# Product 4 of the W_base stage formed for two pairs at once, by seven inner products

## The reference

```
q    = relu(cond @ W3 + b3)                        # one row per batch
y    = relu(((512 * x + sum of x over tokens) * q) @ W2 + b2)
g    = softmax(y @ W_router + b_router); the two largest of 6 are kept
out  = x + y @ W_base + b_base + (y @ A_s) @ B_s + sum over e of g_e * (y @ A_r[e]) @ B_r[e]
```

## Time and profile before

| what | value |
|---|---|
| median of 3 runs | 1394.6 us (1394.54 to 1394.91) |
| profiled execution, first to last instruction (span) | 1392.4 us |
| PE busy | 1388.2 us, 6105 matmuls |
| DVE busy | 986.5 us (71%) |
| ACT busy | 644.2 us (46%) |
| DMA queues | 237.78 MB, mean 171 GB/s |

### The profile page before, as it was taken

One profiled execution on the slowest core, in us unless ns is written; L12 is line 12 of the kernel. 1 busy time (PEld: TensorE's weight loads), 2 busy tenths in 40 slices (PEclk: granted clock), 3 DMA queues, 4 the chain that ended last, 5 costly groups with the idle time before them and its releaser, 6 DMA issues.

```text
span 1392.4 us, 18247 instructions
## 1 busy us (share of the span) xinstructions
PE 1388.2 (100%) x6105; PEld 1142.9 (82%) x6105; DVE 986.5 (71%) x1648; ACT 644.2 (46%) x1190; POOL 60.7 (4%) x136
## 2 busy tenths in 40 slices
PE   9999999999999999999999999999999999999999
PEld 6888888888888888888888888888888888888887
DVE  6987777676786757768889667766667656586663
ACT  7774756657465564655544232431314313243130
POOL 3000110000000000000000001000000000000000
PEclk9999999999999999999999999999999999999999
DMA  8243836445264452546836549556463665635542
GB/s 318 75 168 113 263 122 182 156 122 165 62 184 153 122 165 61 171 130 211 285 92 195 212 132 342 176 190 226 146 239 114 203 213 167 218 107 175 211 155 87
DMA packets 146429, 237.78 MB, mean 171 GB/s; under 512 B 39872, under 2 KB 40128, under 8 KB 146336
## 3 DMA queue, kind: packets, MB, share of 16 engines
q1 hardware_dynamic: 135680, 199.75, 43.6%
q0 software_dynamic: 9792, 35.66, 8.3%
q10 hardware_dynamic: 864, 1.22, 0.2%
HBM read 157.53 MB, written 79.04 MB: 170 GB/s over the span
## 4 chain that ended last, share of the span: by engine, by line
PE 100%; DVE 0%; DVEq 0%; issue 0%
PE ps L2392 33%; PE ps L2393 33%; PE ps L2394 33%; PE ps L2403 1%; PE ps L2418 0%; PE ps L2412 0%; DVE buf L2385 0%; DVEq L59 0%; DVE zeros L1708 0%
## 5 line engine op out<-in xcount | busy, mean ns | idle before, releaser
L2392 PE MATMUL ps<-act_hi,w_hi 128*128 128x512 f32 x1600 | 623.0, 389 | 0.0
L2393 PE MATMUL ps<-act_lo,w_hi 128*128 128x512 f32 x1600 | 622.8, 389 | 0.0
L2394 PE MATMUL ps<-act_hi,w_lo 128*128 128x512 f32 x1600 | 622.8, 389 | 0.0
L2392 PEld LDWEIGHTS ps<-act_hi,w_hi 128*128 128x128 f32 x1600 | 300.4, 188 | 63.1 <-DVE act_lo L1520 0.9
L2393 PEld LDWEIGHTS ps<-act_lo,w_hi 128*128 128x128 f32 x1600 | 300.4, 188 | 62.3
L2394 PEld LDWEIGHTS ps<-act_hi,w_lo 128*128 128x128 f32 x1600 | 300.4, 188 | 62.2
L854 ACT ACTIVATE act_hi<-src 128x512 fp32r<-128x512 f32 x232 | 140.5, 624 | 152.6 <-PE ps L2394 151.5
L1595 DVE SCALAR_TENSOR_TENSOR buf<-ps,bb_sb,buf 128x512 f32<-128x512 f32 x115 | 85.6, 748 | 125.6 <-PE ps L2394 100.7
L1527 DVE TENSOR_TENSOR act_lo<-src,act_hi 128x512 fp32r<-128x512 f32 x192 | 130.2, 685 | 23.8 <-ACT act_hi L854 23.6
L873 ACT ACTIVATE yhi<-buf 128x512 fp32r<-128x512 f32 x128 | 80.1, 626 | 81.3 <-PE ps L2394 80.9
L1595 DVE SCALAR_TENSOR_TENSOR buf<-ps,b_sb,buf 128x512 f32<-128x512 f32 x80 | 59.4, 748 | 43.8 <-PE ps L2394 43.7
(11 more groups left out here) (165 smaller groups left out, 1490.0 us busy)
## 6 DMA issues: line engine op xcount, KB each, us to landing
src<-in_xT SPq DMA_DIRECT2D x224, 256.0 KB, 3.7
y_scratch<-buf SPq DMA_DIRECT2D x128, 256.0 KB, 3.1
src<-y_scratch SPq DMA_DIRECT2D x128, 256.0 KB, 5.2
outT<-buf SPq DMA_DIRECT2D x127, 256.0 KB, 4.6
inner_w<-inner_scratch POOLq DMA_DIRECT2D x42, 512.0 KB, 3.8
buf<-in_xT SPq DMA_DIRECT2D x32, 256.0 KB, 4.9
inner_scratch<-staged_w POOLq DMA_DIRECT2D x14, 512.0 KB, 5.3
wl_raw<-in_wbase SPq DMA_DIRECT2D x7, 1024.0 KB, 5.7
```

Of the source, the lines that this page charges most:

```text
L2392: nc.tensor.matmul(out, wh, a_h, start=start, stop=False, skip_group_check=onto)
L2393: nc.tensor.matmul(out, wh, a_l, start=False, stop=False, skip_group_check=onto)
L2394: return nc.tensor.matmul(out, wl, a_h, start=False, stop=stop, skip_group_check=onto)
```

## The change

In the W_base stage (g = 8 to 15) the three couples of joined pairs now make product 4 together as well. Names: `RUNS` lists the series of seven inner products: r = 0, 1, 2 for the W2 stage, and two for each couple of the W_base stage, one for product 1 (r = 3, 5, 7) and one for product 4 (f = 4, 6, 8). A tile `partner4` (the place of `w_hi[:, 4]`) holds the other pair's tiles, `acc4` (the place of `w_lo[:, 4]`) the sum for C12, `t2_four` is a new buffer. The inner products of product 4 stand on PE among the groups of products 3 and 5, the first behind the second group of product 3; the third and fourth stand back to back. The low-rank terms of C11 and C12 move into the inner products m = 1 and m = 5 of the even pair, and for C12 of the odd pair into the groups of product 3.

The weights of product 4 are no longer there in raw form, so `raw_four` on DVE adds `w_hi` and `w_lo` again (two 128x1024 additions). Seven more weight sets c = 14 to 20 are made and stored: 14 to 18 in the second pair, 19 and 20 in the third (g = 10, `EARLY` = 3 is the index of this pair in `QUADS`).

```diff
+        RUNS = [(e_of, n_of) for e_of in range(len(QUADS)) for n_of in ((1, 4) if e_of >= EARLY else (1,))]
+        RUN = {key: r_of for r_of, key in enumerate(RUNS)}
...
+            def load_x12(p):
+                for j in range(H):
+                    if p > 2:
+                        sp.wait_ge(buf1_stored[j], 16 * 2 * (NP + p - 1))
+                    else:
+                        sp.wait_ge(inner_w_lo, 3 * L2)
+                    sp.dma_start(acc4[:, j, :], xT[2 * p + 1, j]).then_inc(x12_loaded[j], 16)
...
             def store_weights(c):
                 pool.wait_ge(inner_w_lo, c + 1)
...
+            def weights_stored(kind):
+
+                for q in range(2):
+                    pool.wait_ge(inner_w_stored[q], 16 * ((L2 * (kind + 1) + 1 - q) // 2))
...
+            def load_partner4(e):
+                g = QUADS[e] + 1
+                if e == EARLY:
+                    weights_stored(2)
+                for h in range(2):
+                    if e > EARLY:
+                        pool.wait_ge(c12_done, four(QUADS[e] - 1, 2 * h + 1))
...
             for c in range(L2, 2 * L2):
                 store_weights(c)
             for e in range(EARLY, len(QUADS)):
-                begin(e)
+                begin(RUN[e, 1])
                 load_partner(e)
-                stream(e)
+                if e == EARLY:
+                    for c in range(2 * L2, 3 * L2):
+                        store_weights(c)
+                load_partner4(e)
+                stream(RUN[e, 1])
+                begin(RUN[e, 4])
+                stream(RUN[e, 4])
...
             def inner_weight_high(c):
 
                 k = c % L2
-                act.wait_ge(wl_loaded[1], 16 if c < L2 else 48)
+                if c < 2 * L2:
+                    act.wait_ge(wl_loaded[1], 16 if c < L2 else 48)
+                else:
+                    act.wait_ge(inner_w_sum, RAW4)
                 if k >= 3:
-                    act.wait_ge(inner_w_sum, 4 * (c // L2) + k - 2)
+                    act.wait_ge(inner_w_sum, sums_no(c // L2, k - 2))
                 if c >= 2:
                     act.wait_ge(inner_w_stored[c % 2], 16 * (c // 2))
-                nc.scalar.activation(staged_w[:, c % 2, 0], INNER_SETS[k][0], ACT.Copy).then_inc(inner_w_hi, 1)
+                nc.scalar.activation(staged(c)[:, 0], inner_set(c), ACT.Copy).then_inc(inner_w_hi, 1)
...
+                a_max(r)
+                inner_high(r, 0)
+                inner_high(r, 1)
+                if e == EARLY:
+                    inner_weight_high(3 * L2 - 2)
                 copy_p0(g, 0)
...
+                copy_p0(g, 2)
+                if e == EARLY:
+                    inner_weight_high(3 * L2 - 1)
                 for j in range(H):
                     high(g, 2, j)
...
-                    if g == SECOND - 1 and j in (0, 2):
-                        inner_weight_high(L2 + 5 + j // 2)
-                if p < LAST:
-                    for j in range(H):
-                        high(g + 1, 0, j)
+                    if g == SECOND - 1 and j in (0, 1):
+                        inner_weight_high(L2 + 5 + j)
+                    elif g == SECOND - 1:
+                        inner_weight_high(2 * L2 + j - 2)
+                for j in range(H):
+                    high(g + 1, 0, j)
+                    if g == SECOND - 1 and j > 0:
+                        inner_weight_high(2 * L2 + 1 + j)
...
+            def raw_four():
+
+                dve.wait_ge(bank_done, group_no(SECOND - 1, 4, H - 1))
+                for k in (0, 2):
+                    nc.vector.tensor_tensor(wl_raw[:, 4, k:k + 2, :], w_lo[:, 4, k:k + 2, :].bitcast(F32),
+                                            w_hi[:, 4, k:k + 2, :].bitcast(F32), ALU.add).then_inc(inner_w_sum, 1)
...
+            def before_next(p):
...
+                    if g == SECOND - 1 and j == 1:
+                        inner_weight_low(2 * L2 + 2)
+                        inner_weight_sums(2)
+                    elif g == SECOND - 1 and j > 1:
+                        inner_weight_low(2 * L2 + 1 + j)
...
             def even(e):
                 g = QUADS[e]
+                r, f = RUN[e, 1], RUN[e, 4]
+                group(g, 0, 0)
+                inner(r, 0)
+                group(g, 0, 1)
+                group(g, 0, 2)
+                inner(r, 1)
+                group(g, 0, 3)
+                inner(r, 2)
+                group(g, 2, 0)
+                inner(r, 3)
...
+                group(g, 3, 0)
+                for j in range(1, H):
+                    group(g, 3, j)
+                    inner(f, j - 1)
+                inner(f, 3)
+                for j in range(H):
+                    group(g, 5, j, (1, 3 * (g - NP) + 3, hb_hi, hb_lo))
+                    if j < H - 1:
+                        inner(f, H + j)
```

More of the change, by code:

```diff
@@ L388, in adaln_ffn, with inner_tiles @@
         wb_lo_no = lambda n, k: H * WB_LO_ORDER.index(n) + k + 1
+        def inner_tiles(r):
+            if RUNS[r][1] == 1:
+                own, others, t2_half, t3_half = G21, partner, buf2[:, 0:2, :], buf2[:, 2:4, :]
+            else:
+                own, others, t2_half, t3_half = G22, partner4, t2_four[:], src[:, tile(G22, 0):tile(G22, 2), :]
+            return ((src[:, tile(own, 0):tile(own, 2), :], src[:, tile(own, 2):tile(own, 2) + 2, :]),
+                    (others[:, 0:2, :], others[:, 2:4, :]), t2_half, t3_half)
         block = ctx.enter_context(nc.Block())
@@ L1058, in partner_scale, with inner_high @@
                                      accum_out=partner_vsum[:, k:k + 1]).then_inc(partner_scaled, 1)
-            def inner_high(e, m):
+            def inner_high(r, m):
+                e, n = RUNS[r]
                 g = QUADS[e]
+                q = G21 if n == 1 else G22
+                own, others, t2_half, t3_half = inner_tiles(r)
                 maximum = ACT.Copy if e < EARLY else ACT.Relu
-                func, source = ACT.Copy, src[:, tile(G21, 0):tile(G21, 2), :]
+                func, source = ACT.Copy, own[0]
@@ L1421, in odd @@
                         copy_u2(g, j - 1)
+                    if j == 0:
+                        lr_high_b(p)
                 copy_u2(g, H - 1)
+                for j in range(H):
+                    copy_u4(g, j)
+                    high(g, 5, j)
+                for j in range(H):
+                    high(g, 6, j)
+                    if j == 1:
+                        lr_high_d(p)
+                if p < LAST:
+                    for j in range(H):
+                        high(g + 1, 0, j)
             def pair2(p):
                 g = NP + p
-                if not joined(g):
-                    alone(p)
-                elif g in QUADS:
+                if g in QUADS:
                     even(QUADS.index(g))
-                else:
+                    return
+                if joined(g):
                     odd(p)
+                    return
+                alone(p)
                 for j in range(H):
@@ L1953, in even1 @@
+                nc.vector.tensor_tensor(out[:, j, :], ps[:, B_BANKS[jt], :], out[:, j, :], ALU.add
+                                        ).then_inc(done, 1)
             def even1(e):
@@ new lines, in even @@
+                inner_t4(f)
+                c12_bank(p, 2)
+                add_u2(f, 0)
+                inner_low(f, 4)
+                low(g, 5, 0)
+                low(g, 5, 1)
+                low(g, 5, 2)
+                low(g, 5, 3)
+                c12_bank(p, 3)
+                add_u2(f, 1)
+                inner_low(f, 5)
+                u4_add_x(p, 0)
+                u4_add_x(p, 1)
+                inner_low(f, 6)
+                add_u4(f, 0)
+                add_u4(f, 1)
+                u4_add_x(p, 2)
@@ new lines, in even, with c22_of @@
+                u4_add_x(p, 3)
+                c22_of(p, 0)
+                c22_of(p, 1)
+                add_p6(f, 0)
+                add_p6(f, 1)
+                low(g, 6, 0)
+                low(g, 6, 1)
+                lr_low_d(p)
+                c22_of(p, 2)
+                u2_add_x(p, 2)
+                u2_add_x(p, 3)
+                low(g, 6, 2)
+                low(g, 6, 3)
+                u2_add_x(p, 0)
+                u2_add_x(p, 1)
+                c22_of(p, 3)
+            def c22_of(p, j):
+                dve.wait_ge(x22_added, four(p, j))
+                c22(NP + p, j)
@@ L2639, in even, with odd @@
+            def odd(p):
+                g = NP + p
                 for j in range(H):
                     group(g, 0, j)
-                    inner(e, j)
-                for j in range(H - 1):
+                for j in range(H):
                     group(g, 2, j)
-                    inner(e, H + j)
-                group(g, 2, H - 1)
+                    low_rank_c11(p, j)
+                group(g, 3, 0)
+                group(g, 3, 1)
+                low_rank_c12(p, 0)
+                group(g, 3, 2)
+                low_rank_c12(p, 1)
```

(5 more changed lines are left out.)

706 lines of the change are left out of this document (478 added, 228 removed).

## The result

The changed kernel takes 1417.4 us (median of 4 runs, 1416.22 to 1418.14) against 1394.7 for the kernel before on the same chip. The ratio is 1.0160 with a 95% interval of 1.0145 to 1.0174. It is slower, as forecast, but by 22.7 us and not by 13.2: the time lies 1.4 us above the upper end of the range. The profiled execution has a span of 1415.5 us, so 23.1 us have to be accounted for.

What follows compares the result with a forecast made beforehand. PE was taken as the bound, busy 1388.2 of 1392.4 us. The sum was 1394.6 - 8.2 (matmuls) + 1.2 (small waits) + 9.9 and 8.8 (long waits) + 1.5 (clock) = 1407.8 us, range 1396 to 1416, 8 times in 10.

Steps and rivals of the forecast that it cites:

- The 36 matmuls: Three couples: 96 matmuls become 84 in each; at 0.2267 us apiece a gain of 8.2 us if nothing waits.
- Both long waits: PE idle in the third pair, before inner product m = 0 (9.9 us) and before m = 2 (8.8 us); chance 0.62.
- First wait: Third pair's start: late stores of new weight sets delay the operand of inner product m = 0; 9.9 us.
- 884.4 + 1.0 + 1.1, then DVE 1.2: Behind set 18 on ACT: `a_max`, first `inner_high`, then DVE's low part; third pair's operand ready at 887.7, before at 877.82.
- The load of 76% for the couple: DVE in a steady couple: busy about 128 of 168.6 us after the change, up from 113.3 of 171.4; still fits.
- Second wait: Third pair, inner product m = 2: POOL loads its weights only behind stores 14 to 20 and `partner4`; 8.8 us.
- Clock: PE's matmuls slow after idling, charged once behind the wait at m = 2; 1.5 us, bounds 0 and 4.
- Small waits: All three couples: PE waits 0.3 us at product 5 and 0.1 at the odd pair's last low-rank matmuls; 1.2 us.
- The weights of the fourth inner product: Each couple: requested 5.4 us before needed, loads taking 3.6 to 5.9; hidden but for 0.5 us at worst.
- the four terms: Added losses: wait before m = 0 (9.9 us), wait before m = 2 (8.8), clock (1.5), small waits (1.2).
- the last row of the table: Account row for time lost before the third pair (1.1 us) and the rest (0.4): predicted 0, measured 1.5 us.
- The rival with DVE as the bound: All three couples: DVE's in-order list holds PE up, 3 us more per couple, 1416 us; chance 0.09.

Runs made afterwards that it cites:

- run 2: Changed kernel with POOL issuing the third pair's weight loads for m = 2, 3, 4 ahead of stores 19 and 20 and the partner4 loads; 1405.5 us, ratio 1.0069.
- run 4: Changed kernel with weight sets 16 to 20 made inside the third pair and POOL's weight loads for m = 2 to 4 ahead of late stores; 1394.05 us, ratio 0.9988.
- runs 1: Changed kernel without the seven new weight sets, product 4 reading product 1's stored weights (output not the reference's); 1391.8 us, ratio 0.9974.
- run 5: Changed kernel with weight sets 16 to 20 made inside the third pair, but POOL's list left as in the changed kernel; 1411.97 us, ratio 1.0116.

## Why the prediction was off

**What held.** The 36 matmuls are gone, and at 8.2 us for them the account closes within 0.4; DVE is not what bounds the couples (runs 2 and 4). Both long waits are where the prediction put them, from the causes that it named (runs 1, 2, 4, 5), and the slow clock behind the first one is paid within the second (run 2 shows it in the open). The sign was right for more than one reason: with either wait taken away the other still makes the kernel slower than before (runs 2 and 5).

**First wait, 12.1 for 9.9.** Set 13's high part was to stay at 856.49, which should have brought its store forward to 858.1. It waited for the landing of store 11 and came at 858.46; the store went at 860.24, as late as before (860.17). The landing of store 14 was put at 877 and came at 879.9, 1.1 of it by chance. By luck the store two behind it made up for that: store 16 landed in 3.0 us where 5 was taken. ACT's `inner_high` was done at 887.6, as the forecast had it (886.5 and the 1.1). The step that failed is the one behind: "884.4 + 1.0 + 1.1, then DVE 1.2". It gave DVE to the inner operand the moment ACT was done. DVE had the set parts, the tile parts and the sums of 9 us to work off first, and came to it at 889.77. The load of 76% for the couple said nothing of this stretch.

**Second wait, 10.6 for 8.8.** Counted from m = 0, store 20 was put at 11.6 us and came at 12.6, the weights' issue at 18.8 and came at 19.4, and their landing took 6.1 for 5. All three are behind by little, and in the same direction.

**Clock, 2.9 for 1.5.** The price came from the earlier trace rows: nine matmuls in 3.52 us. That was a poor row for it. The row has nine because the kernel issues nine there, so it does not say how long slow matmuls go on. And the granted clock stood at 1.00 there, while here the windows say 0.50 from 916 to 920; what made those nine slow stays open. The price here is 14 steps with 0.2 us lost in each, in run 2 behind the first hole the same 2.9, and in the changed kernel behind the first hole 2.0.

**Small waits, 4.2 for 1.2.** Product 5 was 0.6 late and not 0.3. "The weights of the fourth inner product" were worked out and found in time, as they were; the wait came at the fifth. Its weights fall together with two x tiles and four y tiles, where 6.6 us stand against the 3.8 of the median. The upper bound of 3 for this term was too low, since it counted a landing of at most 5.9 in a kernel whose DMA queues had 18 MB less to move.

**The range.** The errors of the four terms are 2.2, 1.8, 1.4 and 3.0 us, 8.4 in sum and all of one sign; with the last row of the table it is 9.9, against 9.6 between forecast and median. The prediction's own upper bounds were 13, 14.4, 4 and 3, which with the 8.2 of the matmuls make 1394.6 - 8.2 + 34.4 = 1420.8. The range stopped at 1416, as if long and short landings would cancel. They didn't: each term was taken too low for a reason of its own (a backlog on DVE, late stores and landings, a row that was no measure of the clock, a landing under load). The rival with DVE as the bound was summed too low as well: three couples of 3 us are 9 and not 8, which gives 1416.8, still under the measured time.

## What to carry to other kernels

Where a change adds stores and loads to one in-order queue, write down the queue's list and put the time of each entry beside it: what stands behind the last store waits for it, however idle the engine is on average. When a late landing releases an engine, everything queued behind the wait runs then, and the operand that PE needs comes at the end of this backlog, not one instruction later. And where a sum has several uncertain waits, their errors can all have one sign, as here; a range has to reach near the sum of their upper bounds.

## What the runs showed of the hardware

- In the second hole, with PE idle for 8.4 us, the granted clock was 1.00 until 912, then 0.53 (912 to 916) and 0.50 (916 to 920, PE busy again), then 0.88 (922 to 924) and 1.00. That is a fall from 2.4 to 1.2 GHz in the pause, and a return after some 6 us of matmuls started 0.43 us apart. Behind the small waits it stayed at 1.00, but not always: in run 5's third couple PE paused for 1.96 us (1305.19 to 1307.54), went on at 0.23 us a matmul, and fell to 0.43 at 1308.92, for 3 us. The pause of 1.74 us in run 4 had no such sequel.

```profile
1307.00:1309.00 2.00, 1.46 (x6) 1.22 (x7) 0.36 (x1) 0.00 (x0) 0.00 (x0) 0.90 1.06 393
1309.00:1312.00 3.00, 3.00 (x9) 2.33 (x8) 0.00 (x0) 0.00 (x0) 0.00 (x0) 0.50 0.20 76
```

- A pause of PE costs more than its length: behind the small waits of these runs the next matmul comes 0.30 to 0.34 us behind the first and not 0.23, even where the idle time is 0.19.
- Stores of the same 0.5 MB, 11 us apart, landed 9.4 and 3.0 us after issue. The long one fell in a stretch with the DMA share at 1.02, the short one at 0.37. The long one was also issued right behind four loads on the same queue, and no run separates the two.
